# A four-layer graph network on one core: softmax sums from the accumulator, probabilities divided on GpSimd, new orders of work

## The reference

```python
h = jnp.maximum(_layernorm(x), 0.0); x = x + _L0(h, ...)   # attention of 8 heads, masked by adj
    attn = softmax(where(adj == 0, -inf, q k^T * scale)); o = (attn v) w_proj + b_proj
    return o + layernorm(o) * ln_gamma + ln_beta
h = jnp.maximum(_layernorm(x), 0.0); x = x + _L1(h, ...)   # linear attention
    rel = adj.T * (q k^T); rel = rel / norm(rel); return rel v
h = jnp.maximum(_layernorm(x), 0.0); x = x + _L2(h, ...)   # graph attention
    h = x W; e = leaky_relu(s1 + s2.T, 0.2) * adj; att = softmax(e); return elu(att h + beta * h)
h = jnp.maximum(_layernorm(x), 0.0); x = x + _L3(h, ...)   # (adj x) weight + bias
```

## Time and profile before

| | |
|---|---|
| median of 3 runs | 1473.15 us (1472.97 to 1476.63) |
| the profiled execution's own time | 1474.63 us |
| its span, first to last instruction | 1472.8 us |
| mean granted TensorE clock | 0.995 of full |
| matmuls, VectorE, ScalarE, GpSimd busy | 1438.2, 1273.4, 1134.7, 748.4 us |

### The profile page before, as it was taken

How to read it: one execution, slowest core, us unless ns; L and a number is a source line. 1 busy time by engine, 2 the same in 40 slices (tenths; PEclk the granted TensorE clock), 3 DMA queues, 4 the chain that set the end, 5 groups by cost and what they waited for, 6 DMA issues and landing times.

```text
span 1472.8 us, 47814 instructions
## 1 busy us (share of the span) xinstructions
PE 1438.2 (98%) x16136; PEld 1370.3 (93%) x16136; DVE 1273.4 (86%) x5774; ACT 1134.7 (77%) x2884; POOL 748.4 (51%) x1107
## 2 busy tenths in 40 slices
PE   5999999999999999999999999999999999999996
PEld 5899999999999999999999999999999999999985
DVE  4889988988989889889889889889889889889885
ACT  4778878878877877877877778778778788788753
POOL 3455555555555555555555555555555555555452
PEclk9999999999999999999999999999999999999998
DMA  3000000100000000001001000000001001000000
GB/s 111 17 17 23 31 16 30 31 16 31 30 17 31 30 16 31 28 19 31 24 23 30 23 24 30 24 24 31 23 24 30 23 24 30 19 28 31 9 23 30
DMA packets 38113, 39.90 MB, mean 27 GB/s; under 512 B 2416, under 2 KB 37488, under 8 KB 37872
## 3 DMA queue, kind: packets, MB, share of 16 engines
q1 hardware_dynamic: 37872, 36.84, 7.9%
HBM read 20.05 MB, written 16.78 MB: 25 GB/s over the span
## 4 chain that ended last, share of the span: by engine, by line
PE 95%; DVE 1%; ACT 1%; issue 1%; POOL 0%; DMA 0%; SPq 0%; POOLq 0%; ACTq 0%; DVEq 0%
PE bank L314 34%; PE mid L314 15%; PE bank L349 6%; PE mid L358 5%; PE bank L520 5%; PE bank L370 4%; PE mid L458 4%; PE mid L374 4%; PE bank L330 4%; PE mid L488 4%; PE bank L417 4%; PE mid L330 2%; PE mid L349 2%; PE mid L493 1%; PE mid L527 1%
## 5 line engine op out<-in xcount | busy, mean ns | idle before, releaser
L546 ACT ACTIVATE probs<-masked,neg_max 128x128 f32<-128x128 f32 x1024 | 326.3, 395 | 6.3 <-DVE neg_max L716 6.3
L903 POOL TENSOR_TENSOR rstd<-var_eps,minus_half 128x2 f32<-128x2 f32 x320 | 240.9, 753 | 25.5
L716 DVE CUSTOM_DVE_ANT_0 masked<-mid,mask 128x128 f32<-128x128 f32 x1024 | 234.9, 286 | 6.9 <-issue 6.8
L915 POOL TENSOR_TENSOR xb<-x,b_proj_beta 128x512 f32<-128x512 f32 x64 | 81.9, 1279 | 233.9 <-DVE o_res L828 233.9
L901 POOL TENSOR_TENSOR var_eps<-mean_var,eps 128x2 f32<-128x2 f32 x320 | 63.5, 198 | 243.0 <-DVE mean_var L710 242.7
L706 DVE BATCH_NORM_STATS2 stats<-x 128x6 f32<-128x256 f32 x384 | 143.3, 415 | 0.1
L725 DVE TENSOR_SCALAR z<-x,mean_var,rstd 128x256 f32<-128x256 f32 x384 | 134.5, 405 | 7.1 <-POOL rstd L903 6.7
L946 POOL TENSOR_TENSOR h_t_lo<-h_t_full,h_t_hi 128x512 fp32r<-128x512 f32 x64 | 82.0, 1282 | 79.4 <-ACT h_t_hi L629 79.4
L349 PE MATMUL bank<-ident,probs 128*128 128x128 f32 x768 | 117.6, 276 | 4.9 <-ACT probs L546 4.9
L942 POOL TENSOR_TENSOR e_mask<-e_leaky,adj_sb 128x256 f32<-128x256 f32 x64 | 46.8, 731 | 116.2 <-DVE e_leaky L770 116.2
L370 PE MATMUL bank<-probs_t,v 128*32 128x128 f32 x2048 | 104.5, 276 | 0.3 <-issue 0.3
(11 more groups left out here) (156 smaller groups left out, 5725.8 us busy)
## 6 DMA issues: line engine op xcount, KB each, us to landing
x<-in_x SPq DMA_DIRECT2D x64, 256.0 KB, 2.7
out_x<-x SPq DMA_DIRECT2D x64, 256.0 KB, 2.1
w_qkv_sb<-in_w_qkv SPq DMA_DIRECT2D x1, 768.0 KB, 4.4
w_q_sb<-in_w_q SPq DMA_DIRECT2D x1, 256.0 KB, 4.4
w_k_sb<-in_w_k SPq DMA_DIRECT2D x1, 256.0 KB, 4.6
w_v_sb<-in_w_v_t SPq DMA_DIRECT2D x1, 256.0 KB, 5.8
w_proj_sb<-in_w_proj SPq DMA_DIRECT2D x1, 256.0 KB, 6.0
w_gat_x<-in_w_gat SPq DMA_DIRECT2D x1, 256.0 KB, 7.2
```

Source lines behind the costliest of these rows:

```text
L546: last = act.activation(probs[:, r, s], masked[:, r, s], ACT.Exp, scale=-1.0, bias=neg_max[:, r, s:s + 1])
L716: last = dve.tensor_tensor_reduce(out=masked[:, r, s], in0=mid[:, r, s * N:(s + 1) * N], in1=mask[:], scale=1.0, scalar=LARGE, op0=ALU.add ...
L903: pool.tensor_tensor(rstd[:, k], var_eps[:, k], minus_half[:], ALU.pow).then_inc(ln_rstd[k], 1)
```

## The change

- The exponentials of the first layer also give their row sums (`accum_out`, into `sums`). VectorE takes the reciprocals of two row groups at a time, and GpSimd multiplies the probabilities in place by them, before they are transposed.
- The products with ones, the logarithm, the exponential of the inverse sums, and the product of heads and inverse sums are gone. ScalarE copies the high part of the heads straight from PSUM, and VectorE subtracts for the low part.
- The third layer's leaky slope is part of ScalarE's activation out of PSUM (Prelu), and `e_sum` is gone.
- There are nine stages instead of eight. Transposing the probabilities and multiplying them by the values has moved from stage 1 to stage 2, and all later layers one stage further.
- The orders of TensorE, ScalarE, VectorE and GpSimd are written anew, with new users for the PSUM banks.
- The weight fold runs in step 2 instead of step 0; the split of the first weights is made in three parts and stands behind step 0 on VectorE. The fold's two transfers are issued behind `CONSTS`.

```diff
-    STREAMS = 8
+    STREAMS = 9
...
-                            pe.matmul(heads_bank[at, to], v0[:, b, hc * RG + r], probs_t[:, r, s],
-                                      start=True, stop=True, tile_position=(0, r * HD))
-                        for r in range(RG):
-                            at = slice(r * HD, (r + 1) * HD)
-                            last = pe.matmul(sums_bank[at, to], ones[:], probs_t[:, r, s],
+                            last = pe.matmul(heads_bank[at, to], v0[:, b, hc * RG + r], probs_t[:, r, s],
                                              start=True, stop=True, tile_position=(0, r * HD))
...
                     last = act.activation(probs[:, r, s], masked[:, r, s], ACT.Exp, scale=-1.0,
-                                          bias=neg_max[:, r, s:s + 1])
+                                          bias=neg_max[:, r, s:s + 1], accum_out=sums[:, r, s:s + 1])
...
-                    act.activation(ln_sum[:], sums_bank, ACT.Ln).then_inc(ln_sum_ready, 1)
-                    act.wait_ge(ln_sum_ready, done(p2))
-                    wait_before(act, o_norm_ready, p2)
-                    act.activation(inv_sum[:], ln_sum[:], ACT.Exp, scale=-1.0).then_inc(inv_sum_ready, 1)
...
+                    act.activation(o_t_p[0][:].rearrange("p b c n -> p (b c n)"), heads_bank, ACT.Copy).then_inc(o_hi_ready, 1)
...
-                        act.activation(e_sum[:, b], s2_bank[:, b * N:(b + 1) * N], ACT.Identity, bias=hw[:, b, D:D + 1])\
+                        act.activation(e_leaky[:, b], s2_bank[:, b * N:(b + 1) * N], ACT.Prelu, bias=hw[:, b, D:D + 1], alpha=ALPHA)\
...
-                    dve.scalar_tensor_tensor(e_leaky[:], e_sum[:], ALPHA, e_sum[:], ALU.mult, ALU.max).then_inc(e_leaky_ready, 1)
...
-                    dve.tensor_tensor(o_t[:].rearrange("p b c n -> p (b c n)"), heads_bank, inv_sum[:], ALU.mult)\
+                    dve.tensor_tensor(o_t_p[1][:].rearrange("p b c n -> p (b c n)"), heads_bank,
+                                      o_t_p[0][:].rearrange("p b c n -> p (b c n)").bitcast(f32), ALU.subtract).then_inc(o_lo_ready, 1)
...
+                    dve.reciprocal(inv_sums[:, 0:2], sums[:, 0:2]).then_inc(inv_sums_ready[0], 1)
...
-                    pool.tensor_tensor(o_t_p[1][:], o_t[:], o_t_p[0][:].bitcast(f32), ALU.subtract).then_inc(o_lo_ready, 1)
...
+                    pool.tensor_tensor(probs[:, 1], probs[:, 1], inv_sums[:, 1].unsqueeze(2).to_broadcast([128, BC, N]), ALU.mult)\
+                        .then_inc(probs_norm_ready[1], 1)
...
-            run(pe, step, [(0, fold), (2, next_weights), (4, last_weights)])
+            run(pe, step, [(1, first_weights), (1, value_weights), (2, fold), (4, folded_weights),
+                          (2, next_weights), (5, last_weights)])
```

More of the change, by code:

```diff
@@ L298, in step @@
                 if store:
[L299 removed]
+                    i = (par + 8) % 2
                     sp.wait_ge(x4_ready, done(p_out))
                     sp.dma_start(out_pairs[p_out], x4[:, i]).then_inc(x_out[i], 16)
[L303 to L304 removed]
+            for t in range(PAIRS + 8):
+                step(t, t % 2, 2 <= t < PAIRS + 2 - 2, t >= 8)
             for i in range(2):
@@ L418, in step @@
-                    last.then_inc(rel_v_psum, 1)
+                        last = pe.transpose(att_bank[:, b * N:(b + 1) * N], att_norm[:, b], ident[:])
+                    last.then_inc(att_t_psum, 1)
                 if on[1]:
@@ L435, in step @@
[L435 to L438, removed]
-                if on[2]:
[L440 to L445, removed]
@@ L446, in step @@
-                if on[5]:
[L447 to L455, removed]
+                if on[2]:
+                    pe.wait_ge(probs_norm_ready[0], done(p2))
+                    bank_free(pe, (probs_t_ready[1], p2, 1), (h_hi_ready[1], p4, 1), (x3_ready, p7, 1))
+                    transpose_probs(0).then_inc(probs_t_psum[0], 1)
@@ new lines, in step @@
+                if on[3]:
+                    dve.wait_ge(o_psum, done(p3))
+                    dve.tensor_tensor(o[:], pair_rows(o_bank), both(b_proj_bc), ALU.add).then_inc(o_ready, 1)
+                if on[5]:
+                    dve.wait_ge(x2_ready, done(p5, 2))
+                    moments(2, p5, x2[:, i5])
+                if on[3]:
+                    dve.wait_ge(o_ready, done(p3))
+                    moments(LN_O, p3, o)
+                if on[2]:
+                    dve.wait_ge(probs_ready[2], done(p2))
+                    dve.wait_ge(probs_ready[3], done(p2))
+                    dve.reciprocal(inv_sums[:, 2:4], sums[:, 2:4]).then_inc(inv_sums_ready[1], 1)
@@ new lines, in step @@
+                if on[3]:
+                    dve.wait_ge(ln_moments[LN_O], done(p3, 2))
+                    for b in range(2):
+                        last = dve.scalar_tensor_tensor(o_gam[:, b], o[:, b], mean_var[:, LN_O, b, 0:1], gamma_bc[:],
+                                                        ALU.subtract, ALU.mult)
+                    last.then_inc(o_gam_ready, 1)
+                if on[7]:
+                    dve.wait_ge(ln_rstd[3], done(p7))
+                    wait_before(dve, h3_ready, p7)
+                    dve.scalar_tensor_tensor(shift3[:], mean_var[:, 3, :, 0], -1.0, rstd[:, 3], ALU.mult, ALU.mult)\
+                       .then_inc(shift3_ready, 1)
@@ new lines, in step @@
+                if on[6]:
+                    dve.wait_ge(att_ready, done(p6, 2))
+                    dve.reciprocal(att_inv[:], att_sum[:]).then_inc(att_inv_ready, 1)
+                    dve.wait_ge(att_inv_ready, done(p6))
+                    wait_before(dve, att_t_psum, p6)
+                    for b in range(2):
+                        dve.scalar_tensor_tensor(att_norm[:, b], att[:, b], att_inv[:, b:b + 1], beta_ident[:],
+                                                 ALU.mult, ALU.add).then_inc(att_norm_ready, 1)
@@ new lines, in step @@
+                if on[3]:
+                    dve.wait_ge(o_gam_ready, done(p3))
+                    dve.wait_ge(o_res_ready, done(p3))
+                    dve.wait_ge(ln_rstd[LN_O], done(p3))
+                    for b in range(2):
+                        dve.scalar_tensor_tensor(x1[:, i3, b], o_gam[:, b], rstd[:, LN_O, b:b + 1], o_res[:, b],
+                                                 ALU.mult, ALU.add).then_inc(x1_ready, 1)
+                if on[1]:
+                    dve.wait_ge(scores_psum, done(p1))
+                    wait_before(dve, probs_ready[2], p1)
+                    least_masked(2).then_inc(max_ready[2], 1)
@@ L864, in _ @@
+                if on[6]:
+                    dve.wait_ge(x3_ready, done(p6))
+                    moments(3, p6, x3_up[:, i6])
+            run(dve, step, [(1, first_constants), (4, fold_low), (2, next_constants), (2, last_constants)])
         @block.gpsimd
```

638 lines of the change are left out of this document (316 added, 322 removed).

## The result

The changed kernel takes 1490.3 us (median of 4 runs, 1489.41 to 1492.49), against 1473.37 for the kernel before in the same job: a ratio of 1.0108, 95% interval 1.0096 to 1.0121. It is slower, by 1.1%, where 1417 us was forecast, and outside the range.

What follows compares the result with a forecast made beforehand. TensorE's own work was taken to bound the kernel at 22.20 us a step, falling to 21.32. 64 x 21.32 = 1364.5, + 52.0 - 6 + 6 = 1416.5 us of span, rounded to 1417 us; range 1406 to 1448.

Steps and rivals of the forecast that it cites:

- TensorE: Products with ones between the products with the values go: 0.88 us less, 21.32 us a step.
- ScalarE: Logarithm and exponential go (1.27 us), sixteen exponentials give sums (1.9 us more): 18.3 us a step, hidden behind TensorE.
- VectorE's own work: Leaky slope goes (0.34 us), two reciprocals come (0.32 us): 19.7 us a step.
- The room of 1.6 us: What VectorE's 19.7 us leaves free in TensorE's step of 21.32 us; before the change it was 2.4.
- GpSimd: Four multiplications of 1.29 us come, one low part of the heads goes: 3.9 us more, 15.4 us a step.
- Start and end: Fold behind the first scores: 6 us less (bounds 1 and 9); one more stage: 6 us more (bounds 0 and 12).
- A: Case as summed: TensorE still bounds every middle step, 1417 us, from 1406 to 1430; chance 0.70.
- C: Rival: VectorE stands still behind long GpSimd operations everywhere, 22.9 us a step, 1518 us, slower; chance 0.07.
- turning point: In the slower rival, meetings costing more than 2.5 us a step (22.20 - 19.7) make the kernel slower than before.
- five places: VectorE's two normalizations, x1, x_exp and att_norm, each held half of 1.29 us by GpSimd: 3.2 us a step.
- B: Rival: two normalizations meet long GpSimd operations, 1.9 us; VectorE sets 21.7 us a step, 1441 us (1425 to 1455); chance 0.20.
- lower bound of A: The as-summed case with the start 9 us earlier and the end at 0: 1406 us.

Runs made afterwards that it cites:

- version without meetings: Changed kernel with inverse root before blocks 3 and 2's multiplications, x3b ahead of rel_sq, x1 behind block 2's masking: 1418.67 us, ratio 0.9611 against the kernel before.

## Why the prediction was wrong, by its own steps

- **TensorE** (0.88 us a step, 56 us in all): right. 0.87 us in the kernel before without those products; 21.27 us a step in the version without meetings, against 21.32.
- **ScalarE** (18.3 us): 18.06. The slope on ScalarE took 0.36 us, as the biased copy had. Four exponentials with their sums take 1.54 us from the first start to the copy behind them, 0.385 each, not 0.41, by this timeline of the changed kernel:

```profile
843.21 0.39 ACT L562 ACTIVATE probs<-masked,neg_max 128x128 f32<-128x128 f32 x1
843.50 0.19 ACT L562 ACTIVATION_READ_ACCUMULATOR probs<-masked,neg_max 128x1 f32 x1
843.59 0.39 ACT L562 ACTIVATE probs<-masked,neg_max 128x128 f32<-128x128 f32 x1
...
844.75 0.37 ACT L612 ACTIVATE hw<-mid 128x258 f32<-128x258 f32 x1
```

- **VectorE's own work** (19.7 us): right, 19.58 without meetings. The room of 1.6 us was right too. What was wrong is that nothing would use it; see the step that failed, below.
- **GpSimd** (15.4 us): 14.95. A multiplication took 1.04 us, not 1.29. That alone would give 14.4; part of the rest is GpSimd being held in its turn, the squares by 0.17 us and two short additions by 0.28 and 0.23.
- **Start and end** (-6 and +6): without meetings -4.9 (first scores at 15.7, not 20.57) and, from the last scores to the end, 87.7 us against 81.2 before, +6.5. In all, its span of 1417.7 less 64 x 21.27 leaves 56.4 us where 52.0 had been forecast. That this version comes within 2 us of 1417 is in part luck: the 4.4 us are mostly made up for by the step, 0.05 us shorter than forecast. The ninth stage was not run by itself.
- **The step that failed** is VectorE's term in the sum of A: it puts at nothing the time that VectorE stands still beside GpSimd. The runs showed 2.74 us a step of it, which made VectorE's work 22.13 us, the step 22.46 and VectorE the pace instead of TensorE. The time had its place among the rivals, and the choice between them failed with it. C's mechanism was the right one, and it had a chance of 0.07; its turning point of 2.5 us a step lies between the 2.39 that still gave a faster kernel and the 2.74 that gave a slower one. I had put C's five places at half a GpSimd operation each, 3.2 us. Three places met; x_exp and att_norm stood beside short operations only and took 0.66 and 0.35 us, no more than in the kernel before. Two of the three cost more than half: z1 three quarters of x3b, 0.96 us, and z2 1.43 us of two multiplications, since its two operations are held one after the other. B had exactly these two places, at 0.7 to 1.2 us each; it took z2 as one meeting with one multiplication, and left out x1. With 1.43 + 0.96 the two z alone make 2.39 us and a step of 22.1, just what most steps of the run with x1 moved show (22.10).
- What misled me was o_gam in the earlier trace rows, which went on beside a power of 128x2 as if nothing were there. That is so in every run, but it says nothing of an operation of 128x512: z2 in the last version also runs its 0.73 us beside the same short operations. The rule of the Trainium skill (page "SBUF — State Buffer", section "Who interferes with whom": the second to come stands still for the whole instruction) should have got the weight, since the order of the change put two multiplications directly behind the inverse root that z2 waits for. The first multiplication stands right behind that root, VectorE has come to z2 by then, and they met in every middle step. The traces agree with the rule for long operations (2.16, 1.69, 1.23 us). For short ones they agree by half: VectorE is not held by a power of 128x2, but a GpSimd addition of 128x2 takes 0.48 us beside x_exp and 0.43 beside o_gam instead of 0.20.
- A slip without weight: the lower bound of A, with the start 9 us earlier and the end at 0, is 1417 - 3 - 6 = 1408, not 1406.

## What to carry to other kernels

When work moves to GpSimd, look not at its load but at what VectorE does at that moment. A VectorE operation that goes from SBUF to SBUF with scalars, or that reads two SBUF operands, should not be released by the same event as a long GpSimd operation, or just behind one; operations that read PSUM and one SBUF operand (here masking at 0.28 us, low parts and residual sums at 0.68), and statistics of one SBUF operand (0.41), stood beside long GpSimd operations at their usual length. Here moving three rows in two orders was worth about 72 us, more than the products that the change removed (57 us in the run without them).

## What the runs showed of the hardware that was not expected

- Where a VectorE pair lies between two long GpSimd operations, its length is theirs: 2.16 us both for the z that takes 0.73 us alone and for the one that takes 0.48.
- Both sides pay: the squares on GpSimd took 0.78 instead of 0.61 us beside x1, and an addition of 128x2 took 0.48 instead of 0.20 us beside x_exp.
- A GpSimd multiplication of 128x512 by a number repeated 128 times took 1.04 us in place, while a subtraction of two full operands of that size (the low part of h_t1) takes 1.30. Forecast from the 0.62 us of 256 columns had been 1.24 at least.
- A pair of normalizations with two constants runs in 0.48 us, with two scalars from SBUF in 0.73.
